# A decoder layer on one core: the last two steps and the FFN written as one stream, a norm moved by one step, and scores in four quarters

## The chip, the cores and the metric

The kernel runs on one core of a Trainium2 chip. The metric is the device time of one execution in microseconds (us), from runs on the chip; the median of three runs of the kernel before is 426.86 us (426.23 to 427.14). The profile is of one execution. Engines are called as in the profile: PE is the matrix engine (PEld its weight loads), DVE, ACT and POOL are the vector, scalar and GpSimd engines, SP is the queue that issues most DMAs. Each engine works through its own instructions in order and waits on semaphores.

## The reference

One post-norm decoder layer on 16 batches of 128 tokens of width 128, in fp32, with 16 heads of 64:

```python
x = _layernorm(x + self_attention(x, W_Q, b_Q, W_K, b_K, W_V, b_V, W_O, b_O))       # x: (16, 128, 128)
x = _layernorm(x + cross_attention(x, ctx, Wq, bq, Wk, bk, Wv, bv, Wo, bo))         # attends over the 16 heads of one token
x = _layernorm(x + ffn(x))                     # light FFN (64 hidden) + heavy FFN (512 hidden) for all 128 tokens
# cross_attention: scores = einsum('bshd,bsgd->bshg', q, k) / sqrt(64); softmax over g; einsum('bshg,bsgd->bshd', attn, v)
# ffn: rms_norm, @ w1 + b1, exact gelu, @ w2 + b2; a sequence has 128 tokens and 128 are routed to the heavy part
```

## The kernel before

The 16 batches go through a software pipeline of steps. Step s does three things at once: part **a**, the projections, scores and softmax of the self-attention of batch s; part **bc**, the end of the self-attention of batch s-1 (weighted values, output projection, first norm) and the first half of its cross-attention (values, queries, scores); part **d**, the rest of the cross-attention of batch s-2 and its second norm. Four batches make a group, and phase is s modulo 4: in phase 3 and 0 the group's queries and keys are projected (L924 to L926), in phase 0 and 1 the keys of the cross-attention (L944). Steps 3 to 14 are a hardware loop of four steps per turn; 0 to 2 and 15, 16 are written out. Step 16 has only bc and d, step 17 (LAST) only d.

The order of the work is written out by hand, engine by engine, in one `step` function each; what follows is fixed by these lists alone.

- **PE** in a step (L1001): transposes of the probabilities (`transpose_p`, L1043), the value projection (L1099 to L1101), the weighted values (L1110), `scores(0)` (L1051), the output projection (L1133), which waits for both halves of `ot`, the transpose of the cross-attention's probabilities (L951), `scores(1)`, the cross-attention's values (L1151), the transposes of x1 (L1160) and of the normed x2 of the step before (L979), `weighted_v2` (L963), `project_q2` (L1062), more transposes, `project_o2` (L972), the cross-attention's scores (L1231). `scores` issues one product per head: 64 rows (even heads the lower, odd heads the upper half of the array), 128 stationary columns, 128 moving columns.
- **DVE** (L705): `ot` for both halves (L765) with `sums2` (L663, L665) between them in phases 2 and 3, the row maxima of the scores (L720), the first norm (L777, L779, L783, L791) with the block-diagonal products of the cross-attention (L672) inside it, then values and queries of the cross-attention (L735, L713), `stats2`, the choice of each token's own scores (L840, L844) and their maximum (L659). The step ends with `x2_out` (L693, L695, L698), the second norm of batch s-2 and its sum of squares.
- **POOL** (L368): the small powers and sums of both norms (`rstd2`, `rms2`, L358 to L384), the softmax's scaling of the probabilities (L390). `rms2` ends the step.
- **ACT** (L493): copies out of PSUM, the exponentials (L506), `normed_x2` (L467), which scales x2 for the FFN, ahead of the first exponentials of the next step.
- **SP**: for each batch 16 DMAs that spread the cross-attention's values over partitions (L317), once `weighted_v2` of the batch before has read the old ones.

The FFN is done by groups of four batches, each with 5 chunks of hidden units: `up` (L924 to L926, three products of 512 columns), a Gelu on ACT (L490), `down` (L996, four products). Group 0 is woven into step 16. Groups 1 to 3 follow (L1247), with what is left of step 17 between their chunks; there are two PSUM banks for `up`, used in turn. A group ends with one sum (L874), four norms (L880, L884), POOL's power (L413), four scalings (L889) and one DMA of 256 KB (L324). The chunk's hidden units of all groups lie in the same five tiles (`ht`).

Of the kernel before, what the change touches and what calls it, by code (L numbers as in the profile page):

```python
# [34 lines left out]
H, DH = 16, 64  # L35
# [14 lines left out]
def build(nc, x_nat, x_t, ctx_t, w_qk, w_v, w_o, b_qk, b_v, b_o,  # L50
# [10 lines left out]
    with ctx:  # L61
# [34 lines left out]
        warm = sb("warm", [128, 128])  # L96

# [46 lines left out]
        ht = [qt[:, c * GB * T:(c + 1) * GB * T] for c in range(NF)]  # L144
# [25 lines left out]
        X1T, X2T, X2T_IN_LAST_STEP = 7, 0, 6  # L170
# [30 lines left out]
        H_BANK, Y_BANK, X2T_BANK = [0, 1], [7, 6], 2  # L201
# [46 lines left out]
        own_picked, half_set, warm_set = (sem(n) for n in ("own_picked", "half_set", "warm_set"))  # L248
# [8 lines left out]
        def run_steps(eng, step):  # L257
# [8 lines left out]
            for s in range(LAST_LOOPED + 1, LAST):  # L266
                step(s, s // 2, s // GB, s % GB, s < B, 1 <= s <= B, s >= 2)

# [10 lines left out]
        def _(sp):  # L279
# [12 lines left out]

            def step(s, h, g, phase, a, bc, d):
# [12 lines left out]
                if bc:  # L306

                    if d:

                        sp.wait_ge(mm_pv2, 2 * s - 2)  # L310
                    sp.wait_ge(v2s_ready, 2 * s)
                    for pp in range(2):
                        for j in range(J):
                            for ih in range(IH):
                                first = (ih * K * 2 + pp) * J + j
                                col = ((pp * J + j) * IH + ih) * DH
                                sp.dma_start(v2[:, col:col + DH],  # L317
                                             v2s[first:first + (K - 1) * 2 * J + 1:2 * J, :].rearrange("k (g d) -> k g d", g=H)
                                             ).then_inc(v2_moved, 16)

            run_steps(sp, step)
            with sp.Fori(0, B // GB) as g:
                sp.wait_ge(out_ready, g + 1)
                sp.dma_start(out[bass.ds(g * GB, GB)].rearrange("b t d -> t b d"),  # L324
                             x2b[:, bass.ds(g * (GB * D), GB * D)].rearrange("t (b d) -> t b d", b=GB)
                             ).then_inc(out_stored, 16)
            sp.wait_ge(out_stored, 16 * (B // GB))

        @block.gpsimd
        def _(pool):  # L330
# [30 lines left out]

            def rms2(s):
# [5 lines left out]
            def step(s, h, g, phase, a, bc, d):  # L368
# [3 lines left out]
                if a:  # L372

                    pool.wait_ge(in_xres[par], 16 * (h + 1))
                    nc.gpsimd.tensor_tensor(xres[par][:], xres[par][:], bo_row[:], ALU.add).then_inc(xres_ready, 1)
                if bc:
                    pool.wait_ge(mv1_ready, s)
                    nc.gpsimd.tensor_tensor(ve1[:], mv1[:, 1:2], eps[:, 0:1], ALU.add).then_inc(ve1_ready, 1)  # L378
                    pool.wait_ge(ve1_ready, s)
                    nc.gpsimd.tensor_tensor(rs1[:], ve1[:], minus_half[:, 0:1], ALU.pow).then_inc(rs1_ready, 1)  # L380
                    if isinstance(s, int) and s == 1:
                        pool.wait_ge(in_bo2, 16)
                    pool.wait_ge(x1_ready, s)
                    nc.gpsimd.tensor_tensor(x1b[b_par][:], x1[:], bo2_row[:], ALU.add).then_inc(x1b_ready, 1)  # L384
# [16 lines left out]
                if d:  # L401
                    rms2(s)

            run_steps(pool, step)
            for g in range(B // GB):
                if g == 1:
                    over_sum2(LAST)
                    rstd2(LAST)
                    rms2(LAST)
                pool.wait_ge(mv3_ready, g + 1)  # L410
# [5 lines left out]
        def _(act):  # L416
# [76 lines left out]
            def step(s, h, g, phase, a, bc, d):  # L493
# [26 lines left out]
                if static and s == LAST - 1:  # L520
                    f_high(0)
# [25 lines left out]
                if not static or s > 2:  # L547
                    normed_x2(s - 1)
# [793 lines left out]
```

## Time and profile before

| | |
|---|---|
| median of three runs | 426.86 us |
| the profiled execution: its time, its span | 427.01 us, 425.1 us |
| busy: PE, PEld | 399.8 us (94%), 347.2 us (82%) |
| busy: DVE, ACT, POOL | 288.4 us (68%), 239.8 us (56%), 146.9 us (35%) |
| DMA: moved, mean rate | 19.20 MB, 45 GB/s |
| chain that ended last | PE 73%, DVE 16%, ACT 4%, issue 4% |
| from one output projection (L1133) to the next, in the loop | 25.2 us from phase 0 to 1, 18.0 from 1 to 2, 18.4 from 2 to 3, 29.6 from 3 to 0 |
| from the last transposes of step 15's probabilities to the end | 356.5 to 425.1 us |

The profiled execution takes 1.9 us more than its span, and 0.15 us more than the median. A line of the profile's timeline is: start in us, duration in us, engine, line of the kernel, operation, output and inputs, shapes, count; in brackets the idle time of the engine just before and who ended it. Instructions of one kind that follow each other are merged. PE's durations overlap the next instruction, since matrix products are pipelined.

### The profile page before, as it was taken

The numbers are of one execution on the slowest core, as the hardware profiler recorded it, in microseconds if no ns is written. First come the engines' busy times: TensorE is split into PE (matmuls) and PEld (weight loads), VectorE is DVE, ScalarE is ACT, GpSimd is POOL, SyncE is SP. The second block draws the span as 40 slices with busy tenths as digits, with TensorE's granted clock in tenths as the row PEclk, the third lists the DMA queues.
The fourth block names the chain that finished last, engine by engine and source line by source line (L and its number), as shares of the span: only waits on it lengthen the run. The fifth ranks groups of instructions, "written<-read, shape, count | busy, mean of one in ns | idle before, by whom it ended". The sixth has DMA issues, their size and how long they took to land.

```text
span 425.1 us, 14916 instructions
## 1 busy us (share of the span) xinstructions
PE 399.8 (94%) x6068; PEld 347.2 (82%) x6068; DVE 288.4 (68%) x659; ACT 239.8 (56%) x812; POOL 146.9 (35%) x218
## 2 busy tenths in 40 slices
PE   8999899999999999999999999999999998698893
PEld 7797788888998888888988887889888887586772
DVE  4586777775847877668667878658577787437344
ACT  4675575635566565467466747455675565335341
POOL 1542344431414445222424442414234554113022
PEclk9999999999999999999999999999999999999997
DMA  7900113110101112200101022101001101020001
GB/s 276 328 2 8 45 26 90 34 27 8 43 11 30 37 40 70 51 2 17 43 8 46 21 46 76 32 7 36 19 22 39 37 23 47 9 49 25 2 23 53
DMA packets 43594, 19.20 MB, mean 45 GB/s; under 512 B 36544, under 2 KB 40896, under 8 KB 43536
## 3 DMA queue, kind: packets, MB, share of 16 engines
q1 hardware_dynamic: 42688, 16.88, 14.5%
q0 software_dynamic: 560, 1.38, 0.9%
q8 instruction: 48, 0.79, 0.8%
q10 hardware_dynamic: 288, 0.07, 0.1%
q14 instruction: 10, 0.08, 0.1%
HBM read 8.88 MB, written 1.05 MB: 23 GB/s over the span
## 4 chain that ended last, share of the span: by engine, by line
PE 73%; DVE 16%; ACT 4%; issue 4%; POOL 1%; DMA 1%; POOLq 0%; DVEq 0%; SPq 0%; ACTq 0%
PE ps L1133 8%; PE ps L972 7%; PE ps L1062 6%; PE ps L1051 6%; PE ps L944 5%; PE ps L924 5%; PE ps L1043 4%; PE ps L1231 4%; PE ps L926 4%; PE ps L925 4%; PE ps L996 4%; DVE s L844 3%; PE ps L1110 3%; PE ps L963 3%; ACT p L506 2%
## 5 line engine op out<-in xcount | busy, mean ns | idle before, releaser
L506 ACT ACTIVATE p<-ps,neg_max 128x128 f32<-128x128 f32 x256 | 90.0, 382 | 35.9 <-DVE neg_max L720 35.9
L390 POOL TENSOR_TENSOR p<-p,row_inv 128x1024 f32<-128x1024 f32 x32 | 60.7, 1896 | 64.3 <-DVE row_inv L726 64.3
L499 ACT ACTIVATE pt<-ps 128x512 f32<-128x512 f32 x64 | 35.5, 622 | 49.9 <-PE ps L1043 49.9
L506 ACT ACTIVATION_READ_ACCUMULATOR p<-ps,neg_max 128x1 f32 x256 | 57.5, 225 | 0.0
L720 DVE TENSOR_REDUCE neg_max<-ps 128x4 f32<-128x512 f32 x64 | 41.5, 671 | 5.3 <-PE ps L1051 5.3
L1133 PE MATMUL ps<-wo,ot 128*128 128x128 f32 x256 | 32.6, 280 | 6.1 <-DVE ot L765 6.1
L1051 PE MATMUL ps<-kt,qt 64*128 64x128 f32 x512 | 36.9, 284 | 0.0
L1133 PEld LDWEIGHTS ps<-wo,ot 128*128 128x128 f32 x256 | 29.8, 191 | 8.5 <-issue 7.6
L1043 PE MATMUL ps<-ident,p 128*128 128x128 f32 x256 | 35.0, 279 | 1.7 <-POOL p L390 1.3
L765 DVE TENSOR_TENSOR ot<-ps,bv 128x512 f32<-128x512 f32 x32 | 21.5, 673 | 20.8 <-PE ps L1110 19.8
L1062 PE MATMUL ps<-x1t,wq 128*64 128x64 f32 x1024 | 33.8, 224 | 1.9 <-ACT x1t L558 1.1
L1051 PEld LDWEIGHTS ps<-kt,qt 64*128 64x128 f32 x512 | 31.0, 187 | 5.2 <-issue 5.1
L1062 PEld LDWEIGHTS ps<-x1t,wq 128*64 128x64 f32 x1024 | 31.3, 138 | 3.7 <-issue 1.5
L1110 PEld LDWEIGHTS ps<-pt,v 128*64 128x64 f32 x512 | 27.6, 137 | 6.0 <-issue 5.5
L972 PE MATMUL ps<-wo,ot 128*128 128x128 f32 x256 | 31.9, 278 | 0.0
L1043 PEld LDWEIGHTS ps<-ident,p 128*128 128x128 f32 x256 | 27.7, 140 | 4.9 <-POOL p L390 1.7
L1110 PE MATMUL ps<-pt,v 128*64 128x128 f32 x512 | 31.5, 276 | 0.2 <-ACT pt L499 0.2
L972 PEld LDWEIGHTS ps<-wo,ot 128*128 128x128 f32 x256 | 30.2, 192 | 1.8 <-issue 0.3
L378 POOL TENSOR_TENSOR ve<-mv,eps 128x1 f32<-128x1 f32 x16 | 3.0, 189 | 81.6 <-DVE mv L783 81.6
L944 PE MATMUL ps<-cg,wk 128*64 128x128 f32 x512 | 29.7, 274 | 0.0
L713 DVE TENSOR_TENSOR qt<-ps,bq 128x512 f32<-128x512 f32 x32 | 22.1, 689 | 11.3 <-PE ps L1062 11.3
L944 PEld LDWEIGHTS ps<-cg,wk 128*64 128x64 f32 x512 | 27.8, 137 | 1.2 <-issue 0.5
(137 smaller groups left out, 846.6 us busy)
## 6 DMA issues: line engine op xcount, KB each, us to landing
v<-v2s SPq DMA_DIRECT2D x256, 32.0 KB
xg<-x_t SPq DMA_DIRECT2D x4, 256.0 KB, 2.7
pt<-w_qk SPq DMA_DIRECT2D x4, 256.0 KB, 4.7
cg<-ctx_t SPq DMA_DIRECT2D x4, 256.0 KB, 2.8
wo<-w_o SPq DMA_DIRECT2D x2, 512.0 KB, 8.8
out<-x2b SPq DMA_DIRECT2D x4, 256.0 KB, 2.2
xres<-x_nat SPq DMA_DIRECT2D x15, 64.0 KB, 1.8
p<-w_v SPq DMA_DIRECT2D x1, 512.0 KB, 6.3
```

What stands on the lines that cost most here:

```text
L390: nc.gpsimd.tensor_tensor(ph, ph, row_inv[:, 8 * half:8 * half + 8].unsqueeze(2).to_broadcast([T, 8, T]), ALU.mult).then_inc(p_ready, 1)
L499: nc.scalar.activation(pt[:, u * BANK:(u + 1) * BANK], bank(T_BANK[u]), ACT.Copy).then_inc(pt_ready, 1)
L506: last = nc.scalar.activation(p[:, hd * T:(hd + 1) * T], bank(S_BANK[q])[:, pos * T:(pos + 1) * T], ACT.Exp, bias=neg_max[:, hd:hd + 1], a ...
L713: nc.vector.tensor_tensor(qt2[:].rearrange("p (t h) -> p t h", h=H)[:, :, heads], bank(Q2[u]).rearrange("p (h t) -> p t h", h=8), bq2[:, h ...
L720: nc.vector.reduce_max(neg_max[:, first:first + 7:2], bank(S_BANK[q]).rearrange("p (h k) -> p h k", h=4), AX.X, negate=True).then_inc(max_ ...
L944: last = nc.tensor.matmul(bank(BLOCK_BANKS[blk][r])[64 * ih:64 * ih + 64, i * 128:(i + 1) * 128], wk2[:, hd * DH:(hd + 1) * DH], own, star ...
L972: last = nc.tensor.matmul(bank(O2, D), ot2[:, k * 128:(k + 1) * 128], wo2[:, k * D:(k + 1) * D], start=k == 0, stop=k == K - 1)
L1043: last = nc.tensor.transpose(bank(T_BANK[u])[:, i * T:(i + 1) * T], p[:, hd * T:(hd + 1) * T], ident[:])
L1051: mm = nc.tensor.matmul(bank(S_BANK[2 * half + i % 2])[:, (i // 2) * T:(i // 2 + 1) * T], qt[rows, cols], kt[rows, cols], start=True, stop ...
L1062: last = nc.tensor.matmul(bank(Q2[u])[64 * ih:64 * ih + 64, i * HALF:(i + 1) * HALF], wq2[:, hd * DH:(hd + 1) * DH], x1t[:, ih * HALF:(ih ...
L1110: last = nc.tensor.matmul(bank(PV_BANK[u])[64 * (i % 2):64 * (i % 2) + 64, (i // 2) * T:(i // 2 + 1) * T], v[b_par][:, hd * DH:(hd + 1) * ...
L1133: last = nc.tensor.matmul(bank(O, D), ot[:, c * T:(c + 1) * T], wo[:, c * D:(c + 1) * D], start=c == 0, stop=c == NC - 1)
```

## The change

Three parts. (1) `scores`: each product of a head is cut in two by its stationary columns (64 queries each), so that four quarters of the array are used in turn: both halves of the rows, both halves of the columns. The 512 instructions of the profile's count (an fp32 product is two) become 1024. (2) In every step from 3 on, `x2_out(s - 1)` stands behind the first two row maxima of step s instead of at the end of step s-1; `rms2(s - 1)` on POOL stands ahead of the first norm's power, `normed_x2(s - 1)` on ACT behind the first two groups of exponentials; the reciprocal of `sums2` stands behind the second `ot`. (3) Step 16, step 17 and the FFN are taken out of the `step` functions and written as one list per engine, with 20 numbered `up` chunks, 15 `down` chunks and four `down_batch`, up to three banks for `up`, two sets of `ht` tiles, an early activation that only loads the table for the exponentials, and a last group that ends batch by batch: five products, a sum, a norm and a DMA of 64 KB for each.

```diff
-        H_BANK, Y_BANK, X2T_BANK = [0, 1], [7, 6], 2
+        H_BANK = [0, 7, 0, 7, 0, 3, 7, 0, 3, 7, 0, 3, 7, 0, 3, 7, 0, 3, 7, 0]
+        Y_BANK, LAST_Y_BANK = [1, 6, 1], [6, 2, 4, 5]
...
-                        mm = nc.tensor.matmul(bank(S_BANK[2 * half + i % 2])[:, (i // 2) * T:(i // 2 + 1) * T],
-                                              qt[rows, cols], kt[rows, cols], start=True, stop=True)
+                        for qh in range(2):
+                            first = cols.start + qh * HALF
+                            mm = nc.tensor.matmul(bank(S_BANK[2 * half + i % 2])[qh * HALF:(qh + 1) * HALF, (i // 2) * T:(i // 2 + 1) * T],
+                                                  qt[rows, first:first + HALF], kt[rows, cols], start=True, stop=True)
...
 # DVE, in step
                 if a:
                     score_max(0)
                     score_max(1)
+                if not static or s > 2:
+                    x2_out(s - 1)
+                if bc:
+                    stats1(s, b_par)
...
-                if d:
-                    x2_out(s)
...
 # POOL, in step
+                if s_late(s):
+                    rms2(s - 1)
+                if bc:
+                    rstd1(s, b_par)
...
 # ACT, behind the steps
+            f_high(0)
+            for u in (2, 3):
+                act.wait_ge(mm_t, 4 * (B - 1) + u + 1)
+                nc.scalar.activation(pt[:, u * BANK:(u + 1) * BANK], bank(T_BANK[u]), ACT.Copy).then_inc(pt_ready, 1)
+            exp2(B)
...
+            f_high(2)
+            nc.scalar.activation(spare[:], warm[:, 0:1], ACT.Exp).then_inc(spare_set, 1)
+            exp2(LAST)
+            gelu(5)
...
 # DVE, behind the steps
+            f_low(0)
+            attention_out(B, 0)
+            sums2(B)
+            attention_out(B, 1)
+            inverse_sums2(B)
+            values2_out(B, 0, True)
+            values2_out(B, 1, True)
+            x2_out(B - 1)
+            stats1(B, 1)
...
+            for bb in range(GB):
+                sum3_of_batch(bb)
+                if bb:
+                    scale3_of_batch(bb - 1)
+            scale3_of_batch(GB - 1)
...
 # PE, behind the steps
+            transpose_p(B - 1, 2)
+            transpose_p(B - 1, 3)
+            pe.wait_ge(wup_split, 2)
+            pe.wait_ge(pt_ready, 4 * B - 2)
+            up(0)
+            up(1)
+            weighted(B, 1)
...
+            project_o()
+            transpose_p2(B)
+            down(0)
+            up(2)
+            down(1)
...
+            weighted_v2(B, 0)
+            weighted_v2(B, 1)
+            pe.wait_ge(x1t_ready, B)
+            project_q2(B, 0)
+            project_q2(B, 1)
+            up(3)
...
+            scores2(0)
+            up(4)
+            transpose_x2(B - 1, X2T_TAIL[0])
+            project_o2(B)
+            down(2)
+            down(3)
...
+            up(5)
+            down(4)
+            transpose_p2(LAST)
+            up(6)
+            up(7)
+            pe.wait_ge(v2_moved, 16 * 16 * B)
+            weighted_v2(LAST, 0)
...
+            for n in range(10, 15):
+                down(n)
+                up(n + 2)
+            for n in range(17, NF * NG):
+                up(n)
+            for bb in range(GB):
+                if bb == 0:
+                    pe.wait_ge(y_read, NG - 2)
+                down_batch(bb)
```

`up(n)` waits for the low parts of its group's input (`f_low`) and for the Gelu that last read its bank; `down(n)` waits for its Gelu. `down_batch` runs the five chunks of one batch, four of 128 rows and one of 64, into a bank of its own.

## Rows read from the trace of the kernel before

**Rows 1.** The page's first part: busy us, share of the span, instructions.
```profile
PE 399.8 (94%) x6068; PEld 347.2 (82%) x6068; DVE 288.4 (68%) x659; ACT 239.8 (56%) x812; POOL 146.9 (35%) x218
```

**Rows 2.** Waits of PE, 60 to 356 us: us in total, times, longest.
```profile
PE ps L1133 <- DVE ot L765: 2.6, 7, 0.7
```

**Rows 3.** Timeline of step 14 (phase 2): DVE's end of the norm, PE, first norm.
```profile
323.06 0.34 DVE L693 TENSOR_SCALAR x<-t,mv,rs 128x128 f32<-128x128 f32 x1
...
324.19 0.69 DVE L765 TENSOR_TENSOR ot<-ps,bv 128x512 f32<-128x512 f32 x1
...
326.19 2.02 PE L1133 MATMUL ps<-wo,ot 128*128 128x128 f32 x16 [0.26 <-DVE ot L765]
...
328.25 0.29 DVE L777 TENSOR_TENSOR t<-ps,xres 128x128 f32<-128x128 f32 x1 [1.00 <-PE ps L1133]
...
330.25 0.33 DVE L791 TENSOR_SCALAR x<-t,mv,rs 128x128 f32<-128x128 f32 x1
...
330.95 0.27 PE L1160 MATMUL ps<-perm,x 128*128 128x128 f32 x1
```

**Rows 4.** Timeline of step 12: the same end of the norm on DVE.
```profile
299.08 0.34 DVE L693 TENSOR_SCALAR x<-t,mv,rs 128x128 f32<-128x128 f32 x1
...
299.78 0.15 DVE L698 TENSOR_SCALAR ssm<-ss 128x1 f32<-128x1 f32 x1
```

**Rows 5.** Groups by line, PE: count, busy us, mean ns; then idle before.
```profile
L1051 PE MATMUL ps<-kt,qt 64*128 64x128 f32 x512 | 36.9, 284 | 0.0
...
L1062 PE MATMUL ps<-x1t,wq 128*64 128x64 f32 x1024 | 33.8, 224 | 1.9 <-ACT x1t L558 1.1 <-DVE v2s L735 0.9
...
L1231 PE MATMUL ps<-kb,qt 64*64 64x64 f32 x1024 | 18.6, 221 | 0.0
```

**Rows 6.** Waits of PE, 356.5 to 418 us: us in total, times, longest.
```profile
PE ps L996 <- ACT qt L490: 2.9, 2, 1.7
PE ps L1133 <- DVE ot L765: 2.9, 1, 2.9
PE ps L1062 <- ACT x1t L558: 1.1, 1, 1.1
PE ps L1160 <- DVE x L791: 0.8, 1, 0.8
PE ps L924 <- DVE cg_lo L907: 0.7, 1, 0.7
PE ps L951 <- POOL p L353: 0.6, 1, 0.6
```

**Rows 7.** Timeline of the tail: last transposes, DVE behind them, chunks of the FFN.
```profile
356.51 1.09 PE L1043 MATMUL ps<-ident,p 128*128 128x128 f32 x8
...
359.06 0.34 DVE L693 TENSOR_SCALAR x<-t,mv,rs 128x128 f32<-128x128 f32 x1
...
360.14 0.68 DVE L702 TENSOR_TENSOR xg_lo<-xnt,xg_hi 128x512 fp32r<-128x512 f32 x1
...
405.92 1.05 PE L996 MATMUL ps<-wdn,qt 128*128 128x128 f32 x8
...
409.01 0.50 PE L924 MATMUL ps<-cg_hi,wup_hi 128*128 128x512 f32 x1 [0.69 <-DVE cg_lo L907]
...
416.60 1.16 PE L996 MATMUL ps<-wdl,qt 64*128 64x128 f32 x8
```

**Rows 8.** Timeline of SP in step 16: the spread of the values.
```profile
370.16 11.46 SPq L317 DMA_DIRECT2D v<-v2s  x16
```

**Rows 9.** Timeline of DVE behind the last product: sum, scaling.
```profile
417.84 0.69 DVE L874 TENSOR_TENSOR kt<-ps,x2b 128x512 f32<-128x512 f32 x1 [0.50 <-PE ps L996]
...
421.25 1.11 DVE L889 TENSOR_SCALAR x2b<-kt,mv,rs 128x128 f32<-128x128 f32 x4 [1.40 <-POOL rs L413]
```

**Rows 10.** DMA issues: count, KB each, us from issue to landing.
```profile
out<-x2b SPq DMA_DIRECT2D x4, 256.0 KB, 2.2
xres<-x_nat SPq DMA_DIRECT2D x15, 64.0 KB, 1.8
```

More of the change, by code:

```diff
@@ L551, in step @@
                     exponentials(1)
-                if static and s == LAST - 1:
-                    act.wait_ge(in_ffn, 8 * 16)
-                    gelu(0, 0)
-                    gelu(0, 1)
+                if s_late(s):
+                    normed_x2(s - 1)
                 if bc:
@@ L572, in step @@
                     regrouped(s)
-                if static and s == LAST - 1:
-                    for c in range(2, NF):
-                        gelu(0, c)
-                    f_high(1)
                 if a:
@@ L745, in step @@
                     qk_out(0, "B")
-                if static and s == LAST - 1:
-                    f_low(0)
                 if phase == 0 and a:
@@ L894, in _ @@
+            values2_out(B, 1, True)
+            x2_out(B - 1)
+            stats1(B, 1)
+            block_diagonal(B, 0)
+            x1_out(B)
+            block_diagonal(B, 1)
+            f_low(1)
+            regrouped(B)
+            q2_out(B, 0)
+            q2_out(B, 1)
+            pick_own(B)
+            max2(LAST)
+            stats2(B, 0)
+            f_low(2)
+            sums2(LAST)
+            inverse_sums2(LAST)
+            x2_out(B)
             y_out(0)
-            f_low(2)
@@ new lines, in scores2 @@
+            def scores2(phase):
+                for i in range(K * 2):
+                    k, pp = i // 2, i % 2
+                    first = ((phase - 1) % GB * K * 2 + i) * J * H
+                    for ih in range(IH):
+                        rows = slice(64 * ih, 64 * ih + 64)
+                        last = nc.tensor.matmul(bank(S2 + ih)[64 * pp:64 * pp + 64, k * 64:(k + 1) * 64],
+                                                qt2[rows, i * J * H:(i + 1) * J * H], kb[rows, first:first + J * H], start=True, stop=True)
+                last.then_inc(mm_s2, 1)
@@ new lines, in _ @@
+            transpose_x2(B, X2T_TAIL[1])
+            down(5)
+            down(6)
+            pe.wait_ge(xnt_ready, B - 1)
+            project_o2(LAST)
+            up(8)
+            down(7)
+            up(9)
+            down(8)
+            up(10)
+            down(9)
+            up(11)
+            transpose_x2(LAST, X2T_TAIL[2])
+            for n in range(10, 15):
[3 more added lines that the diff above has]
+                up(n)
+            for bb in range(GB):
+                if bb == 0:
+                    pe.wait_ge(y_read, NG - 2)
+                down_batch(bb)
```

471 lines of the change are left out of this document (254 added, 217 removed).

## The prediction

> **What bounds the kernel now.** I read the page's first part, then the waits of PE, then the timelines of the two places where it waits, then the groups by line for what PE does there. PE is busy nearly throughout [rows 1], so only three things can shorten the kernel: a wait of PE, PE's own work, or what runs behind its last product. The waits of PE differ by stage. From step 3 to step 15 there is one of any size: the output projection waits for `ot`, in seven steps, 2.6 us together [rows 2]. From the last transposes of step 15 on there are many: the six listed make 2.9 + 2.9 + 1.1 + 0.8 + 0.7 + 0.6 = 9.0 us [rows 6]. Behind the last product DVE, POOL and the last DMA work alone, from 417.84 us to the end of the span at 425.1 us [rows 9]. These are the stretches that the change touches, and the scores besides.
>
> **Part by part.**
>
> *The norm's end, moved.* In step 14 `x2_out` begins at 323.06 us and the first `ot` follows at 324.19 us: 1.13 us of DVE that stand ahead of what PE waits for, 0.26 us in this step [rows 3]. Taken from there, it frees more than any of the seven waits (the longest is 0.7 us [rows 2]). What is late next is the weighted-values product that `ot` reads, and then the scores, behind which the output projection stands anyway. The block's new place is behind the first row maxima, where DVE idles 1.00 us until the output projection is done [rows 3]. Its length there lies between 1.13 us [rows 3] and the 299.93 - 299.08 = 0.85 us of step 12 [rows 4]; I take 0.85, since at the new place POOL has nothing to do beside it, as POOL waits for this very block. With 0.85 it fits into 1.00; as PE now comes 0.26 us earlier, the first norm is late by 0.1. x1 is written by 330.58 us and PE's transpose of it starts at 330.95 us [rows 3], 0.37 us of slack, of which the earlier PE uses 0.26: just enough. POOL's `rms2`, now ahead of the first norm's power, and `normed_x2` on ACT, behind the first exponentials, are hidden by the same stretch in which DVE does the statistics. Gain between 0 and 2.6 us: I take 2.3.
>
> *The scores in quarters.* Now 512 instructions take 36.9 us: 72 ns each, 144 ns for a pair that uses the two row halves [rows 5]. Then there are 1024, in 256 groups of four that stream the same columns as a pair did. What four quarters cost is seen in the cross-attention's scores, 18.6 us for 1024 instructions of 64 columns, 73 ns for four; two column halves with 64 columns cost 33.8 / 512, 66 ns a pair [rows 5]. So quarters are 7 ns dearer per group than halves, and halves with 128 columns should cost about twice 66. An estimate for the new group is 132 + 7 = 139 ns: 5 ns x 256 = 1.3 us gained. Bounds: 132 ns (3.1 us gained) and 144 + 7 ns (1.8 us lost). I take 1.3, as these rows are of the same form. The doubled weight loads run beside the products, as they do in the cross-attention's scores.
>
> *The tail on PE.* The work is nearly the same, its order is new. Removed: the 9.0 us of waits [rows 6]; between a producer and its consumer there now stands a chunk of the FFN, a Gelu has several banks, and the table for the exponentials is loaded ahead of need. Added, in the order of the list:
> - `up(0)` now stands ahead of the weighted values and waits for `f_low(0)`, which on DVE follows the maximum of step 15, where `x2_out` stood: 359.06 + 0.68 = 359.74 us, against PE's end of the transposes at 357.60 us [rows 7]. A new wait of 2.1 us. Behind it on PE stands everything, first the weighted values, which could have begun earlier; but the two chunks and the values of the cross-attention then cover DVE's work on `ot`, so that the old wait of 2.9 us is not paid as well.
> - `weighted_v2(LAST)` waits for the spread of the last values. Its 16 DMAs start when the `weighted_v2` before is done, take 11.46 us to issue [rows 8] and, by the nearest row of a landing, 1.8 us more [rows 10]: 13.3 us. PE has in between: queries 33.8 / 16 = 2.1, scores 18.6 / 16 = 1.2 [rows 5], the second output projection, of the form of the first, 2.0 [rows 3], three pairs of `up` and `down` at (417.76 - 409.01) / 5 = 1.75, and two more `up` at 1.75 - 1.05 = 0.7 [rows 7]: 12.0 us. So between 0 and 1.3 us; I take 0.6, the middle.
> - The last group ends batch by batch: three more changes to the chunk of 64 rows and back. Such a chunk takes 1.16 us against 1.05 for one of 128 rows [rows 7]: 6 x 0.11 = 0.7 us, between 0 and twice that.
> - Short waits where one result is used soon after (the block-diagonal product, the last queries): 0.3 us, between 0 and 2, the longest single wait of the tail after the two of 2.9 being 1.7 [rows 6].
>
> PE's last product: 9.0 - 2.1 - 0.6 - 0.7 - 0.3 = 5.3 us earlier.
>
> *Behind the last product.* Now from 417.84 to 422.36 us, 4.5 us for four batches [rows 9]. One batch has the instructions of the first norm, which takes 330.58 - 328.25 = 2.3 us from sum to scaling [rows 3]: 2.2 us less. The other three batches are hidden under the products of the next one. The last DMA moves 64 KB instead of 256: 1.8 against 2.2 us [rows 10], 0.4 us less. POOL and SP get more, smaller orders, hidden the same way; if DVE fell behind the products, a batch's 0.3 us of scaling would be added.
>
> *Costed at nothing:* the added memory, the split of `sums2` and its reciprocal (its reader on POOL has a scores product and an output projection of time), the early activation (ACT idles in the tail, as PE's waits for others show).
>
> **Sum.** 2.3 + 1.3 + 5.3 + 2.2 + 0.4 = 11.5 us. The profiled execution took 427.01 us (span 425.1 and 1.9 around it), so 415.5 us; it stands 0.15 us above the median, which gives **415.4 us**.
>
> **Rivals.**
> 1. *x1 becomes the wait.* If the moved block takes 1.13 us, DVE reaches the first norm 0.4 us late while PE has used up its slack, and the transpose of x1 (L1160) waits instead of the output projection. For: the slack is only 0.37 us [rows 3]. Against: the shorter length in step 12 [rows 4]. The 2.3 us go: 417.7 us, and up to 419 where phases 0 and 1, which had no wait, get one.
> 2. *The tail's list runs into its own waits.* PE takes nothing out of order, and DVE, ACT and POOL have lists as long. If the spread lands late and the Gelus queue behind the second table load, new waits eat the 5.3 us: 420.7 us. For: the spread has no spare time. Against: most of the removed waits were for a result issued directly before, which the new order avoids.
> 3. *Slower: the column halves take turns.* The two new quarters of a product have the same rows. If two column halves of one set of rows cannot be loaded and streamed side by side, a group costs two pairs, 288 ns: 256 x 144 ns = 36.9 us more, in the place of 1.3 less, so 415.4 + 38.2 = 453.6 us. It decides above 144 + 10.2 us / 256 = 184 ns a group. Against it: queries of 64 columns, column halves with all rows in common, take 33 ns each, and the cross-attention's scores, in which each set of rows also serves both column halves, 18 [rows 5]. For it: there the row halves alternate with every product, in the new order the column halves do. The Trainium skill (TensorE: Matmul & The Clock Gate, Part 3, what overlaps and what doesn't) says that a weight load overlaps with running products only where the row group differs, which is this rival and by which the time would be this one. By that rule the queries could not take what they take, so the trace here speaks against it.
>
> **How the numbers follow.** The forecast has 0.60; rival 1 0.16, rival 2 0.16, rival 3 0.05, and 0.03 remains for no visible change or a small loss by several new waits. The lower end takes the best bounds: 3.1 for the scores (1.8 more), no waits for the spread, short waits and changes (1.6), 2.6 for the moved block (0.3), that is 411.7, and a little more for waits too short for the list, 411. The upper end takes in rivals 1 and 2: 421.5. About 0.2% (0.85 us) is what a measurement of this kernel can tell from no change. Faster by more than that: forecast, rivals 1 and 2, 0.92; within it 0.02; slower 0.06.
>
> **What would show it.** In the waits of PE between 60 and 340 us, `ot` should be gone and no x1 in its place; in the groups by line the scores should stand at about 35.6 us for 1024. In the tail the first wait should be for `f_low`, about 2 us, then next to nothing until the spread; the last product should end some 5 us earlier beyond the shift of the steps, and sum to scaling of the last batch take about 2.3 us. The prediction is wrong if the scores' group grows, or if x1 or a Gelu heads the list of waits.

## The result, and where the time went

The kernel after takes **413.63 us** (median of four runs, 412.0 to 414.85) beside 427.0 us for the kernel before in the same set of runs; the ratio is 0.9685, 95% interval 0.9644 to 0.9725. Predicted were 415.4 us, so the gain is 13.4 us where 11.5 were forecast. A second set of six runs, told below, gave 413.96 us and a ratio of 0.9663 (0.9626 to 0.9700).

The profiled execution of the kernel after took 414.85 us, the longest of the four, with a span of 413.0, 12.1 us below the span of before. To see where they came from, both traces are cut at three marks: the first output projection (step 1), that of step 15 (the last step in the loop's form), and DVE's last sum. The lines of before that stand at the first two marks are (timeline: start, duration in us, engine, line):

```profile
36.45 1.72 PE L1133 MATMUL ps<-wo,ot 128*128 128x128 f32 x13
...
344.25 2.02 PE L1133 MATMUL ps<-wo,ot 128*128 128x128 f32 x16 [0.32 <-DVE ot L765]
```

and those of after, with DVE's last sum and its last scaling:

```profile
35.72 2.05 PE L1151 MATMUL ps<-wo,ot 128*128 128x128 f32 x16
...
339.35 2.05 PE L1151 MATMUL ps<-wo,ot 128*128 128x128 f32 x16
...
408.95 0.29 DVE L949 TENSOR_TENSOR kt<-ps,x2b 128x128 f32<-128x128 f32 x1 [0.44 <-PE ps L1107]
...
410.72 0.35 DVE L958 TENSOR_SCALAR x2b<-kt,mv,rs 128x128 f32<-128x128 f32 x1 [0.70 <-POOL rs L433]
```

With the sum of before at 417.84 us [rows 9] the four stretches are:

| stretch | before | after | difference | predicted |
|---|---|---|---|---|
| start to the first output projection | 36.45 | 35.72 | -0.73 | 0 |
| to the output projection of step 15 | 307.80 | 303.63 | -4.17 | -3.6 (norm 2.3, scores 1.3) |
| to DVE's last sum | 73.59 | 69.60 | -3.99 | -5.3 |
| to the end of the span | 7.3 | 4.1 | -3.2 | -2.6 (chain 2.2, DMA 0.4) |

The first line is not the change's: in the traces of this study that mark lies anywhere between 35.72 and 36.52 us, in kernels with and without the edits. The waits of PE tell the rest. In the steps (56 to 340 us of the kernel after; us in total, times, longest) the wait for `ot` [rows 2] is gone, and no x1 stands in its place. These two are left:

```profile
PE ps L1015 <- DVE qt L777: 1.4, 3, 0.5
PE ps L1127 <- issue: 0.4, 1, 0.4
```

The first is the wait of the query projections, L924 in before. The change does not touch them, but a PE that comes earlier waits longer there; in before (60 to 356 us) the line is:

```profile
PE ps L924 <- DVE qt L713: 0.9, 2, 0.5
```

From step 15 on the longest waits are now two that the prediction had named, in the place of the six of [rows 6]:

```profile
PE ps L1015 <- DVE xg_lo L740: 2.3, 1, 2.3
...
PE ps L1054 <- DMA v<-v2s: 1.1, 1, 1.1
```

The groups by line show the scores in quarters (before: 36.9 us for 512 [rows 5]):

```profile
L1206 PE MATMUL ps<-kt,qt 64*64 64x128 f32 x1024 | 35.1, 275 | 0.0
```

And the tail shows something that no line of before had: the 32 instructions of the weighted values take 3.21 us here, directly behind PE's wait for `f_low`. The timeline:

```profile
354.75 0.68 DVE L740 TENSOR_TENSOR xg_lo<-xnt,xg_hi 128x512 fp32r<-128x512 f32 x1
...
355.58 0.47 PE L1015 MATMUL ps<-xg_hi,wup_hi 128*128 128x512 f32 x1 [2.29 <-DVE xg_lo L740]
...
357.49 3.21 PE L1139 MATMUL ps<-pt,v 128*64 128x128 f32 x32
...
362.13 1.95 PE L1151 MATMUL ps<-wo,ot 128*128 128x128 f32 x16
```

The stretches around it (from and to, length, PE's busy time and instructions, granted clock, DMA share, GB/s) say why: while PE stands idle the granted clock is full, and for some 3.4 us behind the first chunk it is 0.50, the lower of its two levels (1.2 GHz).

```profile
353.40:355.50 2.10, 0.00 (x0) 1.00 0.25 55
355.50:356.60 1.10, 1.02 (x5) 1.00 0.22 48
356.70:360.00 3.30, 3.30 (x27) 0.50 0.07 16
360.10:363.00 2.90, 2.90 (x25) 1.00 0.00 0
```

### The profile page after: what moved, and what is told of

Same layout as the page of the kernel before. It is cut to its first block, busy times and chain, and to the rows that moved or that the text cites. A ratio compares the mean times of both kernels' runs of the same rounds, so it can differ in the third digit from the quotient of the medians.

```text
span 413.0 us, 15941 instructions
## 1 busy us (share of the span) xinstructions
PE 398.8 (97%) x6580; PEld 344.6 (83%) x6580; DVE 287.6 (70%) x661; ACT 240.1 (58%) x813; POOL 148.1 (36%) x224
## 4 chain that ended last, share of the span: by engine, by line
PE 83%; DVE 6%; ACT 4%; SPq 3%; issue 2%; DMA 1%; POOL 1%; POOLq 0%; DVEq 0%
PE ps L1151 8%; PE ps L1206 7%; PE ps L1139 7%; PE ps L1063 7%; PE ps L1118 6%; PE ps L1127 6%; PE ps L1035 6%; PE ps L1015 5%; PE ps L1017 4%; PE ps L1016 4%; PE ps L1161 4%; PE ps L1054 3%; SPq L309 3%; PE ps L1145 2%; ACT p L535 2%; PE ps L1094 2%
## 5 line engine op out<-in xcount | busy, mean ns | idle before, releaser
L528 ACT ACTIVATE pt<-ps 128x512 f32<-128x512 f32 x62 | 34.5, 625 | 48.7 <-PE ps L1118 48.7
L1206 PE MATMUL ps<-kt,qt 64*64 64x128 f32 x1024 | 35.1, 275 | 0.0
L1139 PEld LDWEIGHTS ps<-pt,v 128*64 128x64 f32 x512 | 28.9, 141 | 6.1 <-issue 6.1
L1139 PE MATMUL ps<-pt,v 128*64 128x128 f32 x512 | 32.7, 282 | 0.0
L1206 PEld LDWEIGHTS ps<-kt,qt 64*64 64x64 f32 x1024 | 27.6, 132 | 5.2 <-issue 5.1
L386 POOL TENSOR_TENSOR rn<-ssm,minus_half 128x1 f32<-128x1 f32 x16 | 8.8, 549 | 55.9 <-DVE ssm L736 55.9
L1015 PE MATMUL ps<-xg_hi,wqk_hi 128*128 128x512 f32 x64 | 26.6, 415 | 1.7 <-DVE qt L777 1.4
```

The source lines that it names most:

```text
L528: nc.scalar.activation(pt[:, u * BANK:(u + 1) * BANK], bank(T_BANK[u]), ACT.Copy).then_inc(pt_ready, 1)
L1015: nc.tensor.matmul(out_cols, w_hi_cols, m_hi, start=True, stop=False)
L1139: last = nc.tensor.matmul(bank(PV_BANK[u])[64 * (i % 2):64 * (i % 2) + 64, (i // 2) * T:(i // 2 + 1) * T], v[b_par][:, hd * DH:(hd + 1) * ...
L1206: mm = nc.tensor.matmul(bank(S_BANK[2 * half + i % 2])[qh * HALF:(qh + 1) * HALF, (i // 2) * T:(i // 2 + 1) * T], qt[rows, first:first + H ...
```

## The experiments

All times are medians; ratios are to the kernel before, run in turn with them, with 95% intervals. The kernel before itself stood at 428.05 to 428.82 us in these sets, so kernels are compared by ratio where it matters.

**The three parts, each alone.** First the scores in quarters, put into the kernel before:

```diff
-                        mm = nc.tensor.matmul(bank(S_BANK[2 * half + i % 2])[:, (i // 2) * T:(i // 2 + 1) * T],
-                                              qt[rows, cols], kt[rows, cols], start=True, stop=True)
+                        for qh in range(2):
+                            first = cols.start + qh * HALF
+                            mm = nc.tensor.matmul(bank(S_BANK[2 * half + i % 2])[qh * HALF:(qh + 1) * HALF, (i // 2) * T:(i // 2 + 1) * T],
+                                                  qt[rows, first:first + HALF], kt[rows, cols], start=True, stop=True)
```

> The kernel before with the scores in quarters and nothing else. My theory (column halves run side by side): the scores' group falls from 36.9 us to 35.1 to 35.6 us for 1024 instructions, and the time by 1.3 to 1.8 us, to 425.0 to 425.5. Rival a (what the scores gain goes into the wait for ot, since the first half of the scores stands directly ahead of the output projection): the group falls as much, the waits of PE for ot grow from 2.6 to about 3.5 us, and the time falls by 0.9 us or less, to 426. Rival b (column halves take turns): the group grows to some 74 us and the time to about 464 us.

Measured: 427.14 us, ratio 0.9973 (0.9960 to 0.9987), that is 0.6 to 1.7 us less. The group stands at 35.1 us, 1.8 us less, so rival b is out. The wait for `ot` grew from 2.6 to 2.8 us (60 to 356 us), not to the 3.5 of rival a:

```profile
L1053 PE MATMUL ps<-kt,qt 64*64 64x128 f32 x1024 | 35.1, 275 | 0.0
```

But between the marks of step 1 and step 15 only 0.94 us are gained (36.51 to 343.37 us): PE's busy time there falls by 1.52 us (301.54 to 300.02), and its idle time grows by 0.58. First before, then this kernel (length, PE's busy time):

```profile
36.45:344.25 307.80, 301.54 (x4927) 1.00 0.14 34
```

```profile
36.51:343.37 306.86, 300.02 (x5377) 1.00 0.14 34
```

The largest part of that growth is the wait of the query projections, 1.4 us in three waits where before has 0.9 in two:

```profile
PE ps L924 <- DVE qt L713: 1.4, 3, 0.5
```

And in the second turn of the loop PE has a new gap, which the profile puts down to issue:

```profile
199.38 0.81 PE L1064 MATMUL ps<-x1t,wq 128*64 128x64 f32 x21 [0.30 <-issue]
```

So rival a was right that a part of the gain goes into a wait, and wrong about which.

Next the end of the norm alone, moved in steps 3 to 15 of the kernel before (with the reciprocal of `sums2` behind the second `ot`, as in the change):

```diff
# DVE, in step (rms2 on POOL and normed_x2 on ACT likewise)
                 if a:
                     score_max(0)
                     score_max(1)
+                if a and (not static or s > 2):
+                    x2_out(s - 1)
...
-                if d:
+                if d and static and s >= B - 1:
                     x2_out(s)
```

> The kernel before with x2_out, rms2 and normed_x2 moved in steps 3 to 15, and nothing else (step 16, step 17 and the FFN as before). My theory: the wait of PE for ot (2.6 us) goes and nothing takes its place: 2.3 to 2.6 us less, 424.2 to 424.6. Rival a (x1 becomes the wait): the transpose of x1 shows waits of 0.2 to 0.3 us a step and the time stays within 0.5 us of 426.9. Rival b (the steps lose more than the listed waits, since gaps too short for the list go too): more than 3 us less, below 424.

Measured: 424.57 us, ratio 0.9923 (0.9905 to 0.9940), 2.6 to 4.1 us less. Between the marks 2.91 us are gained (36.12 to 341.01). From step 2's projection on it is 2.68 us (52.83 to 341.01, before 53.39 to 344.25), close to the 2.6 us of [rows 2], in part by chance: the wait of the query projections grows from 0.9 to 1.4 us here too, and gaps too short for the list are fewer. There is neither a wait for `ot` nor one for x1 from 60 to 340 us, so rival a is out and the mechanism is the predicted one. The time, 3.3 us less by the ratio, would fit rival b as well; the two profiled executions differ by 2.7 us (spans of 425.1 and 422.4).

Then the tail alone: the kernel after with both other parts undone.

> The kernel after with the scores as before (halves) and x2_out, rms2, normed_x2 back at the end of their steps: the tail alone. My theory (the tail is worth 5.3 + 2.2 + 0.4 us by the prediction, 7.3 by the two traces): 419.0 to 419.7 us. Rival (the new order of the tail only pays because the steps ahead of it end earlier, as PE then has the FFN's input sooner): the wait for f_low grows to over 4 us and the time is 421 or more.

Measured: 417.81 us, ratio 0.9770 (0.9732 to 0.9807), better than expected. From step 15's mark to the end of the span it takes 416.9 - 343.56 = 73.3 us, where before takes 80.9 and after 73.7; the wait for `f_low` is the same 2.29 us, so the rival is out: the tail needs nothing of the other two parts. The time varies more than in the other kernels, from 416.36 to 420.87 us. Together the three single gains are 0.27 + 0.77 + 2.30 = 3.3%, and the whole change brings 3.15 to 3.4%: they add.

**Does the order of the quarters matter?** In the change the two column halves of one set of rows follow each other. This kernel lets the row halves alternate instead:

```diff
-                    for i in range(8):
+                    for pair in range(4):
+                        for qh in range(2):
+                            for i in (2 * pair, 2 * pair + 1):
```

> The kernel after with the quarters of the scores in another order: of each pair of heads first the two row halves for the first 64 queries, then the two row halves for the other 64, so that the row halves alternate with every product. My theory (any two of the four quarters run side by side, whatever differs): the scores' group stays at 35.1 us within 0.4, and the time at that of the kernel after (413.6) within 0.8 us. Rival (a load overlaps a running product only where the rows differ): the order of the change would hold up every second load, and with the rows alternating the group falls by more than 1 us and the time to 412.5 or less.

Measured: ratio 0.9679 (0.9660 to 0.9698), 414.6 us; the group is at 35.1 us, the same to the tenth:

```profile
L1207 PE MATMUL ps<-kt,qt 64*64 64x128 f32 x1024 | 35.1, 275 | 0.0
```

So a quarter that follows another of the same rows costs no more than one that follows another of the other rows. This settles rival 3 of the prediction, which had 288 ns a group where 137 are measured. The Trainium skill (TensorE: Matmul & The Clock Gate, Part 3, what overlaps and what doesn't) allows the overlap of a weight load only where the row group differs; by that, this order would have been faster. Another of its pages (TensorEngine Tiling (Array Packing), Key Properties) says that different tiles can load weights and multiply in parallel, and with that the 35.1 us of both orders agree.

**The wait for `f_low` and the clock behind it.** Two kernels ask the same question from two sides. One takes the wait away, by putting the weighted values ahead of the first two chunks of `up`:

```diff
+            weighted(B, 1)
             up(0)
             up(1)
-            weighted(B, 1)
```

> The kernel after with the weighted values of the last batch ahead of the first two chunks of up instead of behind them. My theory: PE has work while DVE prepares f_low, so the wait of 2.3 us shrinks to some 0.6 us (now for the copies of the transposed probabilities), and the granted clock does not fall behind it: 1.7 us less than the kernel after where its clock did not fall (412.0 to 413.0), some 3 us less where it did; median about 410.8. Rival a (the wait moves: the output projection waits for ot or the transpose for x1 as much as was gained): within 0.8 us of 413.6. Rival b (the clock's fall comes from the order of the work and not from the wait): the 3.4 us at half clock are still in the profile, about 412.

The other keeps the wait's end where it is, and fills it with eight products that nobody reads:

```diff
             pe.wait_ge(pt_ready, 4 * B - 2)
+            for i in range(8):
+                nc.tensor.matmul(bank(H_BANK[0], T), ident[:], ident[:], start=True, stop=True)
             up(0)
```

> The kernel after with eight products whose result nobody reads (1.8 us of PE) put into PE's wait for f_low; the wait's end stays where it is. My theory (the granted clock falls because PE stands idle there): no stretch at half clock in the tail in any run, the time that of the kernel after where its clock did not fall, 412.0 to 413.0, median about 412.4. Rival (the fall has another cause, such as the order of the products behind it): the stretch of 3.4 us at half clock stays in the profile, and the median at 413.6.

Measured: the first 411.06 us, ratio 0.9619 (0.9584 to 0.9653); the second 412.84 us, ratio 0.9645 (0.9617 to 0.9672). With the wait filled the chunk begins at the same time as in the kernel after (355.56 and 355.58 us), but the weighted values take 1.97 us instead of 3.21, and the output projection begins at 360.54 instead of 362.13:

```profile
353.20 1.95 PE L1359 MATMUL ps<-ident 128*128 128x128 f32 x16
355.56 0.50 PE L1015 MATMUL ps<-xg_hi,wup_hi 128*128 128x512 f32 x1 [0.41 <-DVE xg_lo L740]
...
357.14 1.97 PE L1139 MATMUL ps<-pt,v 128*64 128x128 f32 x32
...
360.54 1.95 PE L1151 MATMUL ps<-wo,ot 128*128 128x128 f32 x16
```

The granted clock of the same stretch is now full:

```profile
356.70:360.00 3.30, 3.30 (x39) 1.00 0.12 26
```

From chunk to projection that is 6.55 us against 4.98: where the clock falls it costs **1.57 us**, and it falls because PE stood idle, not because of the work behind it. The other traces with this order of the tail bear the price out: the same stretch takes 6.34 to 6.55 us in five further ones where the clock falls, and 4.95 us in the one where it does not, with the same wait of 2.29 us ahead of it (the kernel with a tile of its own, below). So the idle stretch is needed and does not suffice. The clock does not fall in every execution. Of the ten timed executions of the kernel after in both sets, four had a mean granted clock of 0.998 or 0.999 and took 412.0 to 413.1 us; six had 0.992 to 0.994 and took 413.8 to 415.1. With the wait filled all six had 0.997 to 0.999 and took 412.6 to 413.5. That the fall is in the tail is seen in two of these six, the profiled ones; for the other four it is inferred, as the mean also takes in the end of the span, where PE has nothing left to do. Across the traces: of the ten kernels whose tail has a PE wait of 2.3 to 2.9 us (for `f_low`, or for `ot` as in before), eight show such a stretch at half clock, which begins between 0.3 us before the wait's end and 1.4 us behind it; the kernel before as profiled [rows 6] and one other do not. Of the four without such a wait none does. The Trainium skill (TensorE: Matmul & The Clock Gate, Part 1, what's actually happening) says that the chip's watch on TensorE's activity runs freely and does not start with the kernel, so that the same program meets it differently each time; that agrees with six of ten. No run here shows that watch itself.

With the values first, the waits of PE behind step 15 are these two, and rivals a and b are both out for the traced execution (one of its six executions, at 414.05 us, still had a mean clock of 0.994; there is no trace of it):

```profile
PE ps L1054 <- DMA v<-v2s: 0.9, 1, 0.9
PE ps L1139 <- ACT pt L613: 0.5, 1, 0.5
```

**The spread of the last values.** In the kernel after SP issues it only when `weighted_v2` of the batch before has read the tile (timeline of SP, then of PE):

```profile
368.25 11.78 SPq L309 DMA_DIRECT2D v<-v2s  x16
```

```profile
381.40 1.16 PE L1054 MATMUL ps<-pt,v 64*64 64x64 f32 x64 [1.10 <-DMA v<-v2s]
```

This kernel lets it write to the tile of the keys' weights, which is read for the last time some steps earlier, and drops the wait for `weighted_v2`:

```diff
-            spread_values2(B, True)
+            spread_values2(B, True, wk2)
...
-            weighted_v2(LAST, 0)
-            weighted_v2(LAST, 1)
+            weighted_v2(LAST, 0, wk2)
+            weighted_v2(LAST, 1, wk2)
```

> The kernel after with the spread of the last batch's values written to a tile of its own (one that is no longer read), so that its 16 DMAs need not wait for weighted_v2 of the batch before. My theory: they start some 5 us earlier, the wait of PE for v2 (1.1 us) goes, and the time falls by 1.0 to 1.1 us, to about 412.5. Rival (behind the spread stands another result that is as late, such as the block-diagonal products or the table load's exponentials): a wait of nearly 1 us takes its place and the time stays within 0.4 us of 413.6.

Measured: 412.71 us, ratio 0.9649 (0.9619 to 0.9679). The DMAs now begin at 361.11 us, some 7 us earlier, and the wait for them is gone; behind it stands a smaller one for the block-diagonal product, 0.37 us:

```profile
361.11 10.37 SPq L309 DMA_DIRECT2D wk<-v2s  x16
...
378.73 1.16 PE L1054 MATMUL ps<-pt,wk 64*64 64x64 f32 x64 [0.37 <-DVE pt L710]
```

So 0.7 us of the wait of 1.1 are won. The time does not show it well: 0.9 us by the medians, with overlapping intervals, and a part of that is the clock. Executions of like mean clock differ by less: four at 0.997 to 0.999 have a median of 412.4 us where the kernel after has 412.6, two at 0.994 took 413.95 where it has 414.4. The profiled execution shows no stretch at half clock although its wait for `f_low` is 2.3 us; it is the other exception counted above.

**The end batch by batch.** The kernel after with the last group ended as a whole, `up` and `down` in turn as in before:

```diff
-            for n in range(10, 15):
+            for n in range(10, NF * NG):
                 down(n)
-                up(n + 2)
...
-                down_batch(bb)
+                if n + 2 < NF * NG:
+                    up(n + 2)
# and one sum, four norms and one DMA of 256 KB behind it
```

> The kernel after with the last group ended as a whole, as before: up and down in turn, one sum, four norms, one DMA of 256 KB. My theory (by the prediction's terms 2.2 + 0.4 - 0.7): 1.9 us more, by the two traces' ends (from the last sum to the end of the span 7.3 us before, 4.1 after, less 0.6 to 1.2 us for the chunks of 64 rows) 1.9 to 2.6 us more: 415.5 to 416.2. Rival (PE loses with the four separate batches what DVE and the DMA gain): within 0.8 us of 413.6.

Measured: 415.82 us, ratio 0.9705 (0.9673 to 0.9737), some 2 us more. Its last sum begins at 407.86 us and the span ends at 415.1, 7.3 us later (before 7.3, after 4.1), so the ending is worth 3.2 us. PE pays for it: from the last `project_o2` to the last sum it takes 407.86 - 384.50 = 23.36 us there and 408.95 - 384.45 = 24.50 us in the kernel after, 1.14 us more. The rest, 2.1 us, is the gain.

**The changes to the chunk of 64 rows.** In the kernel after the last group's products go 8, 2, 8, 2, 8, 2, 8, 2 (instructions of 128 and of 64 rows in turn), which makes seven changes. Taking the chunk of 64 rows first in every second batch leaves four, so it saves three, and not the four of the expectation:

```diff
-                for c in range(NF):
+                order = range(NF) if bb % 2 == 0 else [NF - 1] + list(range(NF - 1))
+                for c in order:
```

> The kernel after with the chunk of 64 rows taken first instead of last in the second and the fourth batch of the last group, so that PE changes between 128 and 64 rows four times less. My theory (0.11 us a change in the prediction; by the trace of the kernel after a batch takes 1.50 us where ten instructions of 0.11 us would be 1.1): 0.4 us less, up to 0.8, so 412.8 to 413.2 against 413.6. Rival (the change of rows costs nothing and the batch's length is the start of a new accumulation in another bank): within 0.2 us of 413.6, and a batch still takes 1.50 us in the trace.

Measured: 413.17 us, ratio 0.9636 (0.9607 to 0.9666), which overlaps with the kernel after, so the time alone decides nothing. The trace does. From the first product of the last group to DVE's last sum it takes 408.67 - 403.24 = 5.43 us:

```profile
403.24 1.05 PE L1108 MATMUL ps<-wdn,kt 128*128 128x128 f32 x8
...
404.22 0.71 PE L1108 MATMUL ps<-wdl,kt 64*128 64x128 f32 x4
...
404.86 2.05 PE L1108 MATMUL ps<-wdn,kt 128*128 128x128 f32 x16
...
406.84 0.71 PE L1108 MATMUL ps<-wdl,kt 64*128 64x128 f32 x4
...
407.48 1.16 PE L1108 MATMUL ps<-wdn,kt 128*128 128x128 f32 x8
...
408.67 0.29 DVE L949 TENSOR_TENSOR kt<-ps,x2b 128x128 f32<-128x128 f32 x1 [0.24 <-PE ps L1108]
```

In the kernel after it is 408.95 - 402.93 = 6.02 us:

```profile
402.93 1.05 PE L1107 MATMUL ps<-wdn,kt 128*128 128x128 f32 x8
...
403.91 0.48 PE L1107 MATMUL ps<-wdl,kt 64*128 64x128 f32 x2
...
404.33 1.16 PE L1107 MATMUL ps<-wdn,kt 128*128 128x128 f32 x8
```

That is 0.59 us for three changes, 0.20 us each, and it agrees with the 1.14 us that the six further changes of the separate batches cost in the experiment before this one. The rival (the start of a sum in a new bank) is out, since those starts are still there.

**The three edits together**, values first, the tile of its own and the chunk order:

> The kernel after with three edits together: the weighted values ahead of the first chunks of up, the last spread in a tile of its own, and the chunk order of the experiment beside this one. My theory (the three act on different waits, so they add: 411.06 with the first alone, 0.9 for the second, 0.4 for the third): 409.6 to 410.0, with no wait of PE above 0.6 us behind step 15. Rival (with f_low's wait covered, DVE is the next bound and the second edit's gain is lost in a wait for the block-diagonal products or for x1): 410.6 or more.

Measured: **410.73 us** (410.02 to 411.49), ratio 0.9585 (0.9554 to 0.9617), faster than both kernels. No wait of PE above 0.5 us is left behind step 15, as my theory had it. But the time is the rival's (410.6 or more), and a part of its mechanism is there: PE waits 0.4 us for the block-diagonal product where the kernel with the first edit alone waits 0.9 for the spread. From step 15's mark to the end it takes 408.9 - 340.25 = 68.7 us, 0.8 less than with the first edit alone (409.0 - 339.49 = 69.5). The sum hoped for is missed by 0.7 to 1.1 us by the medians; by the ratios (0.9585 against 0.9619, 1.5 us) it is not, so the time does not decide. In the traces the 0.8 us are lost again in the loop, whose gap is 1.02 us here, against 0.2 us with the first edit alone:

```profile
198.03 0.81 PE L1128 MATMUL ps<-x1t,wq 128*64 128x64 f32 x21 [1.02 <-issue]
```

**Are the quarters worth it, then?** The same kernel with the scores in halves:

> The kernel of the three edits together (410.73) with the scores in halves again instead of quarters. What is open: the quarters took 1.8 us from the scores' group but only some 1.1 us from the time of the kernel before, and every kernel with quarters shows a gap of PE put down to issue in the loop's second turn (0.2 to 1.0 us at the queries of the cross-attention), while those with halves show at most 0.2. My theory (the doubled instructions bring the gap): the gap is gone, the scores' group is back at 36.9 us, and the time is 0.3 to 1.2 us above that of the kernel with quarters, 411.0 to 411.9. Rival a (the gap has nothing to do with the quarters): it stays at 0.4 us or more, and the time is 1.8 us above, 412.5. Rival b (with halves ot or x1 becomes late, now that PE is otherwise without waits): a wait of PE for ot in the steps, and more than 1.8 us above.

Measured: 411.37 us, ratio 0.9607 (0.9574 to 0.9641): 0.6 us more by the medians, as my theory had it, though the intervals overlap. The group is back at 36.9 us, a step of the loop from phase 1 to 2 takes 0.12 us more (17.69 against 17.57), and the gap is gone; from 60 to 340 us one wait is left:

```profile
PE ps L1015 <- DVE qt L777: 1.4, 3, 0.5
```

Every kernel with quarters shows the gap at the cross-attention's queries in the second turn, 0.2 to 1.0 us; of the four with halves none does. So this gap comes with the 1024 further instructions of PE (products and weight loads) and takes back a part of the 1.8 us. Gaps put down to issue as such are not the quarters' alone: with the tail alone, in halves, PE has one of 0.27 us at the same products in step 15. What PE waits for in it, no view of the profile shows. Instructions are moved by DMA, and the page's third part has more of that with quarters than with halves. First the kernel after:

```profile
q8 instruction: 52, 0.85, 0.8%
```

Then the kernel with halves:

```profile
q8 instruction: 48, 0.79, 0.8%
```

The Trainium skill (Runtime: NRT & Kernel Launch, Instruction fetch mechanics) says that each engine's sequencer fetches its next block of instructions by its own DMA queue while it works through the present one. That a late block makes the gap is possible, and not shown.

**The kernel after once more**, unchanged, beside the others:

> The kernel after once more, unchanged, beside the others on one chip, since the medians of the kernel before have moved by 0.4 per cent from one set of runs to the next. By the first set its ratio to the kernel before is 0.9685 (0.9644 to 0.9725); my theory has the same ratio within 0.002, in some executions the 3.4 us at half clock in the tail, and a gap put down to issue of 0.2 us or more in the loop. Rival (the first runs were lucky): a ratio above 0.9725.

Measured: 413.96 us, ratio 0.9663 (0.9626 to 0.9700), so the rival is out; its trace has the same two long waits (2.3 and 1.0 us), half clock around the end of the first, and a gap of 0.4 us.

## Why the prediction held, term by term

- **The norm's end, 2.3 us.** Right, and slightly low: 2.7 us in the steps whose waits were counted, 2.9 with the step ahead of them, 3.3 by the time of the part alone. The block at its new place takes from 323.09 to 323.94 us, the 0.85 us that were taken, so DVE reaches the first norm in time and x1 (rival 1) never waits. What the term left out, the growth of the query projections' wait by 0.5 us, was made up by gaps too short for the list.
- **The scores, 1.3 us.** The size of the group was predicted as 35.6 and is 35.1 us: 137 ns a group of four, where 139 were estimated, so 1.8 us. What the prediction lacked is that the whole gain need not reach the time: it put at nothing the next wait, that of the query projections for DVE's `qt` (0.5 us more), and it had no row for the gap put down to issue (0.3 us). 1.15 us arrive in the time. Two errors of opposite sign, so that the 1.3 is luck in part.
- **The wait for `f_low`, 2.1 us.** It is there, 2.29 us, at the place foretold. The step that failed is its price: it was taken as its length alone. In six of ten executions some 1.6 us come on top, through the clock (traced in two of them). [rows 6] gave no hint: the wait of 2.9 us in the profiled execution of before happened to leave the clock alone.
- **The spread, 0.6 us.** Mis-sized: 1.1 us. The sum of the prediction itself gave 13.3 - 12.0 = 1.3 as an end and I took the middle between that and 0, though nothing spoke for 0. Issue and landing took 381.40 - 368.25 = 13.15 us, almost the 13.3 of the working.
- **The chunk of 64 rows, 0.7 us.** Low: 0.20 us a change and not 0.11, so 1.2 us for six; measured are 1.14 us for the separate batches, within the bounds given (0 to 1.4).
- **Short waits, 0.3 us.** About right: the block-diagonal product 0.2 us; a gap of 0.5 us put down to issue in step 15 of the profiled execution is not of this kind.
- **PE's tail, 5.3 us.** 3.99 us by the profiled pair; with the 1.57 us of the clock and the 0.5 us of that gap added back, 6.1. What was counted as removed, 9.0 us, held in full, and rival 2 (a list that runs into its own waits) did not come about. But the terms as measured would give only 9.0 - 2.3 - 1.1 - 1.1 - 0.2 = 4.3. The stretch from step 15's mark to the last sum, first of before and then of after (length, PE's busy time), shows what is missing:

```profile
344.25:417.84 73.59, 64.03 (x836) 1.00 0.09 23
```

```profile
339.35:408.95 69.60, 65.48 (x856) 0.98 0.12 30
```

PE's idle time falls from 9.56 us, 0.6 more than the list of [rows 6] had, to 4.12. Its busy time rises by 1.45 us, though the clock and the changes of rows bring 1.57 + 1.14 = 2.7. So the rest of the work takes some 1.3 us less than before. The prediction had that work as "nearly the same"; what made it shorter is not shown.
- **Behind the last product, 2.2 + 0.4 us.** 3.2 us: sum to scaling takes 411.07 - 408.95 = 2.1 us (2.3 foretold), 2.4 less than before, and from there to the end of the span it is 0.8 us shorter, not 0.4. The 1.8 us for 64 KB came from another DMA's row [rows 10]; the four DMAs that store the last group's results take 1.5 us, 0.7 less than the 2.2 of before:

```profile
out<-x2b SPq DMA_DIRECT2D x4, 64.0 KB, 1.5
```

The prediction held by its mechanism: the waits that it removed are gone, those that it added stand where it put them, and no rival came about. How close its sum is to the profiled pair is luck in part: the three stretches that the change touches bring 4.17 + 3.99 + 3.2 = 11.4 us, where 11.5 were forecast, because the costs without a row (the clock, the gaps put down to issue) and the terms that were too low (the spread, the changes of rows) are met by PE's shorter work in the tail, a cheaper end and cheaper scores. The 13.4 us of the medians are more than that pair shows, as two of the four executions kept the full clock. Without the clock's fall the change would have been worth some 0.8 us more (412.84 us with the wait filled).

## What to carry to other kernels

A wait of the matrix engine costs its own length and, where the clock falls upon it, a slow stretch besides: here 2.3 us cost 3.9 where it fell, in some six of ten executions. And a PE that is made faster in one place may only reach its next wait sooner: of the 1.8 us that the scores gained alone, up to 0.5 went into the wait of the query projections. When chunks of other work are woven into a chain, put ahead of each wait the work whose inputs are ready first; swapping two entries of the list here brought 2.6 us more, a fifth of what the whole change had brought. And price the end of a kernel as a stretch of its own, down to the end of the span: batch by batch it cost PE 1.1 us and returned 3.2.

## What the runs showed of the hardware that was not expected

- PE's clock fell to half for some 3.4 us around or behind the end of an idle stretch of 2.3 to 2.9 us, in eight of ten traces; in the kernel after it fell 1.1 us after the work had begun again. Eight products that nobody reads, put into the idle stretch, kept it at full.
- Four instructions on the four quarters of the array take 137 ns together for 128 moving columns, in either order of rows and columns; a pair, each on half the rows and all columns, takes 144 ns [rows 5].
- A change between products of 128 and of 64 rows costs PE 0.20 us (0.59 us for three).
- Twice the instructions for the scores bring a gap of 0.2 to 1.0 us in the loop's second turn, in ten traces of ten, which the profile can put down to nothing but issue; none of the four with halves has it.
